# One core, two transformer layers in fp32: halved maxima around the weighted output, and FFN and first-batch steps reordered

## The reference, cut to what matters

```python
# layer 0, attention: 4 groups g of 4 heads n, 32 columns each; k and v are the context
q = rope(rms_norm(layernorm(x)) * wq); k = rope(rms_norm(ctx) * wk)
scores = einsum('bgnqd,bgkd->bgnqk', q, k) * scale      # causal
attn = softmax(scores); out = einsum('bgnqk,bgkd->bgnqd', attn, v)
x = x + out @ w_out.T
# layer 0, FFN: rows of the router choose 2 of 8 low-rank experts
gate = h @ W_gate + lora + expert_lora(w); up = ...     # h = layernorm(x), 1376 wide
x = x + (silu(gate) * up) @ W_down + lora + expert_lora(w)
# layer 1: kv = ctx @ W_k.T + b_k; p = layernorm(x) @ kv; sim = p @ kv.T / sqrt(512)
x = x + softmax(layernorm(sim) * gamma + beta)
# layer 1 experts: top 8 of 64, 128 places each
x = x + sum_k w_k * expert_k(x)
```

## Time and profile before

| | |
|---|---|
| median of 3 runs | 1270.76 us (1270.14 to 1270.92) |
| the profiled execution | 1271.93 us, its span in the profile 1270.1 us |
| mean granted TensorE clock | 0.985 of full speed |
| places in the span | PE's line 2448 resumes after its wait for HID at 127.36 (FFN 0), 342.05, 558.61 and 775.18 us (FFN 3) |

### The profile page before, as it was taken

How to read it: one execution, slowest core, us unless ns; L and a number is a source line. 1 busy time by engine, 2 the same in 40 slices (tenths; PEclk the granted TensorE clock), 3 DMA queues, 4 the chain that set the end, 5 groups by cost and what they waited for, 6 DMA issues and landing times.

```text
span 1270.1 us, 19545 instructions
## 1 busy us (share of the span) xinstructions
PE 1192.1 (94%) x6589; PEld 864.8 (68%) x6589; DVE 724.8 (57%) x1476; ACT 525.2 (41%) x1198; POOL 488.3 (38%) x541
## 2 busy tenths in 40 slices
PE   7998999999999999999999999999899999999980
PEld 4667777667877766777776687777566666666650
DVE  7967565686778578687867866655622222222220
ACT  5864222786322278632247843222332333333220
POOL 1431243462233446123453702121355555565630
PEclk9999999999999999999999999999999999999995
DMA  8012231003233000423300023534789999999847
GB/s 298 4 70 76 103 110 63 2 1 123 90 140 106 33 1 12 148 101 104 128 1 1 34 104 141 217 104 170 256 284 348 353 346 352 354 351 356 205 60 142
DMA packets 45922, 187.04 MB, mean 147 GB/s; under 512 B 6732, under 2 KB 9804, under 8 KB 31380
## 3 DMA queue, kind: packets, MB, share of 16 engines
q1 hardware_dynamic: 30980, 146.18, 30.7%
q0 software_dynamic: 14864, 39.85, 13.7%
HBM read 155.31 MB, written 34.90 MB: 150 GB/s over the span
## 4 chain that ended last, share of the span: by engine, by line
PE 77%; DVE 9%; ACT 6%; issue 2%; POOL 2%; DMA 1%; SPq 0%; DVEq 0%; POOLq 0%; ACTq 0%
PE PS L2613 14%; PE PS L2030 11%; PE PS L2032 11%; PE PS L2031 11%; PE PS L2629 4%; PE PS L2120 3%; ACT P L905 3%; PE PS L2633 3%; PE PS L2139 3%; DVE NM L1446 2%; PE PS L2603 2%; PE PS L2049 2%; PE PS L2430 1%; PE PS L2431 1%; PE PS L2622 1%
## 5 line engine op out<-in xcount | busy, mean ns | idle before, releaser
L2613 PE MATMUL PS<-WE,XGT 128*128 128x384 f32 x512 | 192.7, 499 | 1.5 <-DVE HM L2004 0.8
L722 POOL CAST HH<-HID 128x512 fp32r<-128x512 f32 x44 | 37.5, 852 | 323.9 <-DVE HID L1832 323.9
L1034 ACT ACTIVATE WHI<-WRAW 128x1280 fp32r<-128x1280 f32 x44 | 56.0, 1272 | 244.1 <-DMA WRAW<-in_ffn 244.1
L2030 PE MATMUL PS<-XTH,WHI 128*128 128x512 f32 x352 | 140.7, 400 | 0.0
L905 ACT ACTIVATE P<-PS,NM 128x512 f32<-128x512 f32 (+3 forms) x256 | 131.7, 532 | 15.8 <-DVE NM L1446 15.7
L2032 PE MATMUL PS<-XTH,WLO 128*128 128x512 f32 x352 | 138.2, 393 | 0.0
L2031 PE MATMUL PS<-XTL,WHI 128*128 128x512 f32 x352 | 138.0, 392 | 0.0
L2613 PEld LDWEIGHTS PS<-WE,XGT 128*128 128x128 f32 x512 | 87.1, 190 | 56.7 <-issue 21.5
L2011 DVE COPY HMT<-PS 128x256 f32<-128x256 f32 x64 | 27.2, 425 | 163.9 <-PE PS L2622 163.9
L1446 DVE TENSOR_REDUCE NM<-PS 128x2 f32<-128x1024 f32 (+2 forms) x96 | 98.3, 1040 | 30.7 <-PE PS L2039 30.4
L2120 PE MATMUL PS<-ident,P 128*128 128x128 f32 x640 | 94.2, 279 | 11.8 <-ACT P L905 5.5
(11 more groups left out here) (341 smaller groups left out, 2737.8 us busy)
## 6 DMA issues: line engine op xcount, KB each, us to landing
WE<-in_we SPq DMA_DIRECT2D x64, 1152.0 KB, 8.1
WRAW<-in_ffn SPq DMA_DIRECT2D x44, 1060.0 KB, 5.0
acc<-HN SPq DMA_DIRECT2D x17, 256.0 KB, 6.4
out<-X SPq DMA_DIRECT2D x4, 1024.0 KB, 4.9
out<-acc POOLq DMA_DIRECT2D x1, 4096.0 KB, 22.9
hx<-HN SPq DMA_DIRECT2D x3, 1152.0 KB, 4.5
XIN<-in_x SPq DMA_DIRECT2D x3, 1024.0 KB, 5.3
CTX<-in_ctx SPq DMA_DIRECT2D x4, 256.0 KB, 2.9
```

The costliest lines, as they stand in the source:

```text
L1034: act.activation(WHI[slot][:, 0:WD], WRAW[slot][:, 0:WD], ACT.Copy).then_inc(S["wg_hi"], 1)
L2030: pe.matmul(dst, a[0], b_[0], start=first, stop=False, **kw)
L2613: mm = pe.matmul(bank(2 + s % 2, 0, 2 * F1), XGT[s % 2][:, k, :], WE[s][:, k * 2 * F1:(k + 1) * 2 * F1], start=(k == 0), stop=(k == KC - 1))
```

## The change

- **Maxima.** In groups 2 and 3 of every attention unit 4's maximum is taken in two instructions of two heads, one ahead of `normalise(g - 1)` and one behind it, and ACT's exp of the first two heads waits for the first alone. In group 2 the copy of the next group's KST goes ahead of `maximum(2, 5)`.
- **FFN, all four.** In `down_first` the low part (HL) of the ranks and of rows 2 and 3 goes ahead of the wait for `hid_ready`; behind it each of rows 0 and 1 takes its high and low parts together.
- **FFN of batch 0.** ACT normalises rows 0 and 1 ahead of copying KV and rounding chunk 0's weights, and copies out the transposes of rows 0 and 1 ahead of the rounding of the next weights; DVE takes XTL of rows 0 and 1 ahead of chunk 0's WLO.
- **Batch 0's preparation and attention.** DVE computes the row shift ahead of the first keys; the last addition of the other groups' keys comes behind the first two maxima; part 0 of the queries of groups 2 and 3 comes behind the copy of unit t = 1's transposes instead of ahead of it; PE's transposes of the context for layer 1 (`context_T`) go ahead of the last transposes of group 3.

POOL and SP keep their order.

```diff
+    SPLIT_UNIT, MAXIMA = 4, MU + 1
...
-                act.wait_ge(S["s_max"], 1 + MU * gi + i + 1)
+                act.wait_ge(S["s_max"], 1 + MAXIMA * gi + (i + 2 if i > SPLIT_UNIT else i + 1))
                 for n in range(n0, n0 + nh):
+                    if i == SPLIT_UNIT and n == HPG // 2:
+                        act.wait_ge(S["s_max"], 1 + MAXIMA * gi + i + 2)
...
+                if b > 0:
+                    key_columns(b)
+                    first_weights()
+                act.wait_ge(S["shift_ready"], 1 + 2 * b + 1)
+                normed(0)
+                normed(1)
+                if b > 0:
+                    weights_ahead()
+                else:
+                    key_columns(b)
+                    first_weights()
+                turned(0)
+                turned(1)
+                if b == 0:
+                    weights_ahead()
...
+            row_shifts()
             dve.wait_ge(tables_loaded, TABLES_LOADED)
...
-            sig(first_keys(HD, CKV, (XW, QA, QB)), "k_ready", 1)
-            dve.wait_ge(setup_loaded, SETUP_LOADED)
+            first_keys(HD, CKV, rest_spare)
...
-                def maximum(g, i):
+                def maximum(g, i, part=None):
 
                     gi = a * G + g
                     t, n0, nh, at, width = MAX_UNITS[i]
+                    if part is not None:
+                        nh = nh // 2
+                        n0, at = n0 + part * nh, at + part * nh * width
...
+                else:
+                    sig(key_rows(HD, CKV, rest_spare), "k_ready", 1)
+                    dve.wait_ge(setup_loaded, SETUP_LOADED)
                 for g in range(G):
...
-                    if g > 0:
+                    if g > 1:
+                        maximum(g, 4, 0)
                         normalise(g - 1)
-                    maximum(g, 4)
+                        maximum(g, 4, 1)
+                    else:
+                        if g > 0:
+                            normalise(g - 1)
+                        maximum(g, 4)
...
+                    if g == G - 2:
+                        stack(g + 1, 0, KST)
                     maximum(g, 5)
                     if g < G - 1:
-                        if not sims:
+                        if g < G - 2 and not sims:
                             stack(g + 1, 0, KST)
...
-                    query_part(g + 2, 0)
...
                     turned(g, 1, 0, 2)
+                    query_part(g + 2, 0)
...
-                wg_rest(0, 0)
+                if b > 0:
+                    wg_rest(0, 0)
                 turned_rest(0)
+                if b == 0:
+                    turned_rest(1)
                 shifts(b, 2, 2, 4)
-                turned_rest(1)
+                if b > 0:
+                    turned_rest(1)
+                else:
+                    wg_rest(0, 0)
...
+                    if not tail and g == G - 1:
+                        context_T()
                     turn(g, 0, 0, 4)
...
+                    pe.wait_ge(S["hl_ready"], 1 + b * NF + 1)
+                    ranks_down(HL[0], hi)
+                    for t in (2, 3):
+                        rows_down(t, HL[0], hi)
                     pe.wait_ge(S["hid_ready"], 1 + b * NF + 2)
                     for t in (0, 1):
                         rows_down(t, HH[0], hi, lo)
-                    pe.wait_ge(S["hl_ready"], 1 + b * NF + 1)
-                    ranks_down(HL[0], hi)
-                    for t in range(NT):
                         mm = rows_down(t, HL[0], hi)
                     mm.then_inc(S["dn_ps"], 1)
```

More of the change, by code:

```diff
@@ L1023, in keys_values, with key_columns @@
                 act.activation(KVT[:, :], KVT[:, :], ACT.Identity, bias=key_shift[:, 0:1]).then_inc(S["kv_act"], 1)
+            def key_columns(a):
                 act.wait_ge(S["kv_ps"], 1 + a + 1)
@@ L1034, in wg_hi @@
                     act.activation(WHI[slot][:, 0:WD], WRAW[slot][:, 0:WD], ACT.Copy).then_inc(S["wg_hi"], 1)
-                act.wait_ge(S["op_ps"], 1 + NT * b + 1)
-                wg_hi(0, 0, b * N0 + 1)
                 def wd_hi(slot):
@@ L1051, in turned, with first_weights, weights_ahead @@
                         "p (k q) -> p k q", k=KC), ACT.Copy).then_inc(S["xT_hi"], 1)
[L1052 to L1064, removed]
+                def first_weights():
+                    act.wait_ge(S["op_ps"], 1 + NT * b + 1)
+                    wg_hi(0, 0, b * N0 + 1)
+                def weights_ahead():
+                    act.wait_ge(S["dn_ps"], 1 + b * NF)
+                    wd_hi(0)
+                    wg_hi(1, 1, b * N1 + 1)
+                if b > 0:
[13 more added lines that the diff above has]
+                    weights_ahead()
+                act.wait_ge(S["shift_ready"], 1 + 2 * b + 2)
+                normed(2)
+                normed(3)
+                act.wait_ge(S["cov_ps"], 1 + b + 1)
+                act.activation(COV[:, :], bank(0, 0, P), ACT.Copy, scale=1.0 / T).then_inc(S["cov_sb"], 1)
+                turned(2)
+                turned(3)
                 if b > 0:
@@ L1284, in per_tile, with key_parts, first_keys @@
                 return table[:, :, b0:b1].unsqueeze(2).broadcast_to([P, NT, n, b1 - b0])
-            def first_keys(c0, c1, spare, between=lambda: None):
-                n, width = (c1 - c0) // HD, NT * (c1 - c0)
-                raw, ka, kb = (sp[:, 0:width].rearrange("p (t c) -> p t c", t=NT) for sp in spare)
+            def key_parts(c0, c1, spare):
+                return (sp[:, 0:NT * (c1 - c0)].rearrange("p (t c) -> p t c", t=NT) for sp in spare)
+            def first_keys(c0, c1, spare):
+                n = (c1 - c0) // HD
+                raw, ka, kb = key_parts(c0, c1, spare)
                 def parts(ap, a, z):
@@ L1299, in first_keys, with key_rows @@
                 fstep.post(turned(ka, 0, HD, ck, 0, HD))
-                between()
                 fstep.post(turned(kb, ROT, HD, sk, 0, ROT))
                 fstep(turned(kb, 0, ROT, sk, ROT, HD))
+            def key_rows(c0, c1, spare):
+                _, ka, kb = key_parts(c0, c1, spare)
                 return dve.tensor_tensor(KR[:, :, c0:c1], ka, kb, ALU.add)
@@ L1346, in row_shifts @@
                 assert fstep.n == FIRST["scaled"], fstep.n
+            row_shifts()
             dve.wait_ge(tables_loaded, TABLES_LOADED)
-            dve.wait_ge(S["f_out"], 1 + 1)
-            fstep(first_keys(0, HD, [XN[:, 3, i * P:(i + 1) * P] for i in range(3)], row_shifts))
+            first_spare, rest_spare = [XN[:, 3, i * P:(i + 1) * P] for i in range(3)], (XW, QA, QB)
+            first_keys(0, HD, first_spare)
+            fstep(key_rows(0, HD, first_spare))
             assert fstep.n == FIRST["keys"], fstep.n
@@ L1446, in maximum @@
                     dve.tensor_reduce(NM[:, t * HPG + n0:t * HPG + n0 + nh], src, AX, ALU.max,
-                                      negate=True).then_inc(S["s_max"], 1)
+                                      negate=True).then_inc(S["s_max"], 2 if i == SPLIT_UNIT and part is None else 1)
                 def turned(g, t, n0, nh=1):
@@ L2296, in attention @@
                     if g == G - 1:
-                        context_T()
                         if tail:
+                            context_T()
                             projected_out(1, 1, 2)
@@ L2655 @@
 KSTEPS = {"f_dve": 35, "f_more": 11, "g_dve": 1, "g_pool": 5}
-FIRST = {"scaled": 22, "keys": 25}
+FIRST = {"scaled": 19, "keys": 25}
 def shape_constants():
```

## The result

The changed kernel took 1262.14 us (median of 4 runs, 1261.57 to 1262.62), the kernel before on the same chip 1270.84 (1270.14 to 1271.27): a ratio of 0.9932, with a 95% interval of 0.9918 to 0.9946. The forecast was 1261.6, range 1259.0 to 1264.8. The profiled execution took 1262.62, with a span of 1260.8 against 1270.1.

A forecast was written before the change was run, and what follows sets the result against it. PE, busy 94% of the span, was taken as the bound, except DVE in batch 0's first groups. Gaps closed summed to 9.2 us, taking the 1270.76 median to 1261.6; own range 1260.2 to 1263.0, 8-in-10 range 1259.0 to 1264.8.

The forecast's parts named there:

- The sum: Whole kernel: all predicted gains added, 9.2 us off the median of 1270.76, giving 1261.6.
- term 2: Groups 2 of three attentions: halved maximum and earlier KST copy shorten PE's waits, 0.75 us each, 2.3 in all.
- term 4: Start of batch 0: row shift computed ahead of the first keys, 0.77 us earlier; bounds 0.4 and 0.8.
- Term 1: down_first, four FFNs: three HL matmuls fill PE's wait for HID, 0.69 us each, 2.8 in all; 0.4 gap stays.
- Term 3: Groups 3 of three attentions: ACT's wait of 0.19 us for the maximum is won, 0.6 in all.
- Terms 5 and 6: Batch 0's attention: keys' addition behind two maxima, 0.2 us; query parts behind the copy in two groups, 1.0.
- Terms 7 and 8: Batch 0: context_T moved into PE's wait for ACT, 0.45 us; new order at FFN 0's start, 1.1.
- XTL's two leads: Start of FFN 0: first XTL 2.04 us earlier by the edit, the third about 0.8.
- The rival of the lock: Batch 0, group 2: DVE's copy RDB slips ahead of POOL's acL, saving 1.76 us more, 1259.8; chance 12%.
- twelve collisions: Attentions with a tail: RDB behind a POOL instruction costs 1.76 us each time; all 12 give 1282.7; slower case 3%.
- The gains that don't arrive: A later wait in each batch (weights, lists) takes gains up: under 2.5 us in all, 1269; chance 5%.

The follow-up runs named there:

- the parts that were run alone: Kernel before with one part each: down_first 1269.63 us, maxima 1269.44, batch 0's preparation and attention 1269.68, start of FFN 0 1270.73.
- the part alone: Kernel before with the new order of down_first alone, in all four FFNs: 1269.63 us, ratio 0.9987.

## Why the prediction was right, point by point

- **The sum.** Predicted 9.2, found 10.1 in the places named, of which 8.6 were left at 905 us; 0.7 more came from the clock. The medians moved by 8.7 us. The mechanisms stood, but for KST in term 2 and the lower bound of term 4, and the parts that were run alone give nearly the same in their own places. That the total came within 0.5 us is partly luck: the places gave 0.9 more than predicted, and the medians show 1.4 less than the places. The medians of the parts run alone (6.2) are not explained by these terms.
- **Term 1**: 0.69 for each, confirmed by the part alone; the gap left is 0.1, not 0.4, since three of the four waits had been 0.83 and not 1.02 us, and I had read the longest. That of FFN 1 shrank by 0.2 through batch 0's part, which no term had.
- **Term 2**: 0.73 for 0.75. Right for the halves; the part ascribed to KST is wrong, its effect is -0.09.
- **Term 3**: 0.30 for 0.19, mis-sized: I had priced ACT's wait ahead of its first exp alone. That exp now begins 0.76 us behind the start of ACT's copies (285.89 to 286.65) where it was 1.06 (291.11 to 292.17): the wait of 0.19 and 0.11 more, because an exp that needn't wait starts before the copy's end in the trace. PE's wait for P in that group fell from 0.56 to 0.20.
- **Term 4**: the size looks right (0.95 for 0.77) and isn't the edit's alone: 0.65 are, 0.30 are the input's. Kernels that keep the old place of the row shift had a lead of 0.95, 1.09, 0.78, 0.56 and 0.30 at the first scores: the profiled execution of before had started late, by its transfers (finv done at 11.06, in those five between 10.20 and 10.64) and by the longest way from finv to the shift, 0.81 us, where those five have 0.63, 0.41, 0.59, 0.76 and 0.10. The filling wasn't on its path (PE waited 0.99 for the keys). What failed is "0.77; bounds 0.4 and 0.8" read from one execution: the lower bound should have been nothing, since the shift had sometimes been early already, and behind a long filling the edit is hidden (from finv to the scores 8.73, 9.00 and 9.40 in the three such traces with the new place, 8.95, 9.07 and 9.30 in the three with the old). What it gives on average isn't settled.
- **Terms 5 and 6**: 1.26 for 1.2, together; no run has the one without the other. That DVE is full there, the reason given for taking so little of term 5, is what the clock's return without a gain showed.
- **Terms 7 and 8**: 0.54 for 0.45 (0.44 and 0.34 in the other two traces) and 1.25 for 1.1. XTL's two leads came out to 0.02 us.
- **The rival of the lock** didn't happen, and its price was wrong by five times: 0.36 and not 1.76 a collision in batch 0, because the next thing on DVE waits for PE anyway. By that price twelve collisions (4.3 us) would not have made the kernel slower; what one costs in a tail no run shows. It was the price of the instruction, and should have been that of the next one that anybody waits for.
- **The gains that don't arrive**: 1.4 us of 10.1 did not in the first trace, 0.86 by a late transfer and the rest in small steps, and 0.6 of 10.2 in the second. The transfer was late in one execution of three, so it isn't shown to be of the change's making.

## What to carry to other kernels

A wait on the engine that bounds can be filled with matmuls whose data is already there, and a whole instruction can be cut in two when its consumer starts with the first half; both give what the timeline says, to 0.1 us. Before such a cut is copied to the next place, ask who waits for the instruction that it is put around: the same edit gave 0.8 us in groups 2 and cost 1.2 in groups 1. Read a gain at the start of a program from several executions, or give it a lower bound of nothing.

## What was not expected of the hardware

One program ran the same stretch at a mean granted clock of 0.58 in one execution and 1.00 in another (22 to 26 us), and the idle time of PE just ahead of it does not tell them apart: PE had been idle for 1.91 us and kept the clock in the changed kernel's first trace, for 1.91 and lost it in its second and with acL behind woL, for 2.48 and kept it with `down_first` alone, for 2.48 and lost it in the kernel before. The pace of the first matmuls changed from 0.43 to 0.21 us at 7.86 to 10.85 us, from execution to execution, under a granted clock shown as 1.00; 512 columns in 0.43 and in 0.21 us are 1.2 and 2.4 columns per ns, the two levels of the clock.
